# Causal attention with 16 heads on Trainium2: softmax row sums by TensorE over four key tiles in place of GpSimd additions and one product

## What is computed

```python
def _L2_attn_ref(x, w_q, w_kv, w_o, k_weights):      # h = 16 heads, v = 64 values per head
    q = x @ w_q * (1.0 / jnp.sqrt(d))                # (b, 512, 1024) -> (b, 16, 512, 64)
    kv = x @ w_kv                                    # keys and values from one projection
    k = kv * (1.0 + k_weights)
    logits = jnp.einsum('bhik,bhjk->bhij', q, k)
    logits = jnp.where(tril, logits, -1000000.0)     # causal
    a = jax.nn.softmax(logits, axis=-1)
    y = jnp.einsum('bhij,bhjv->bhiv', a, kv)
    return y @ w_o
...
x = _layernorm(x + _L2_attn_ref(x, ...))
```

## Time and profile before

| | us |
|---|---|
| median of 3 runs | 3564.88 |
| lowest and highest of them | 3562.05, 3566.03 |
| profiled execution, its own time | 3560.01 |
| its span in the trace | 3558.3 |
| TensorE matmuls busy | 2880.4 (81%) |
| VectorE busy | 2106.9 (59%) |
| ScalarE busy | 1306.5 (37%) |
| GpSimd busy | 882.6 (25%) |
| first and last exponential of the stage (line 2372) start at | 2013.0 and 2456.9 |

### The profile page before, as it was taken

The page is one execution under the profiler, slowest core; times in us unless marked ns, Lnnn a source line. Parts: engine busy times, 40 slices in busy tenths (PEclk is TensorE's granted clock), DMA queues, the critical chain, the costliest instruction groups (busy, mean ns, idle before and its releaser), DMA issues. The chain is left out here.

```text
span 3558.3 us, 41277 instructions
## 1 busy us (share of the span) xinstructions
PE 2880.4 (81%) x14768; PEld 1337.2 (38%) x14768; DVE 2106.9 (59%) x4175; ACT 1306.5 (37%) x2243; POOL 882.6 (25%) x1147
## 2 busy tenths in 40 slices
PE   4996879665555998879797899997785599699998
PEld 1332434221112443535354434434333233254555
DVE  5874841478777545555555355555667678464444
ACT  2664642333432552020211243332553266355221
POOL 2101100257546103030303254445215200110000
PEclk9997889888777999889899899999786699799999
DMA  5212200100001200000000000000300221220000
GB/s 136 42 28 59 47 19 1 47 0 0 0 0 31 60 12 1 1 1 0 1 1 1 17 1 1 1 1 1 61 12 0 34 42 34 73 51 8 1 1 12
DMA packets 39979, 74.60 MB, mean 21 GB/s; under 512 B 13048, under 2 KB 31916, under 8 KB 35936
## 3 DMA queue, kind: packets, MB, share of 16 engines
q1 hardware_dynamic: 39776, 71.96, 9.3%
HBM read 26.28 MB, written 1.05 MB: 8 GB/s over the span
## 5 line engine op out<-in xcount | busy, mean ns | idle before, releaser
L1630 POOL TENSOR_TENSOR mamba_dbu<-mamba_du,mamba_b 128x512 f32<-128x512 f32 x128 | 256.0, 2033 | 134.1 <-ACT mamba_b L1613 134.1
L1597 PE MATMUL ps<-mamba_hc,weights 128*128 128x512 f32 x256 | 167.1, 745 | 97.1 <-DVE mamba_hc L1655 96.7
L1644 DVE TENSOR_TENSOR_SCAN mamba_h<-mamba_da,mamba_dbu 128x512 f32<-128x512 f32 x128 | 211.3, 1653 | 18.3 <-ACT mamba_da L1618 18.3
L164 POOL TENSOR_SCALAR vareps<-mv 128x4 f32<-128x4 f32 x24 | 6.1, 254 | 760.6 <-DVE mv L1271 463.0
L534 DVE TENSOR_REDUCE L3a_negmax<-ps 128x1 f32<-128x512 f32 x256 | 162.5, 684 | 52.1 <-PE ps L294 51.6
L2310 DVE TENSOR_REDUCE skv_negmax<-ps 128x2 f32<-128x256 f32 (+3 forms) x128 | 105.1, 823 | 147.4 <-PE ps L2158 147.4
L534 DVE TENSOR_REDUCE L0a_negmax<-ps 128x1 f32<-128x512 f32 x256 | 162.5, 684 | 50.1 <-PE ps L294 49.6
L397 ACT ACTIVATE L0a_probs<-ps 128x512 f32<-128x512 f32 x256 | 143.7, 599 | 76.1 <-PE ps L313 74.5
L397 ACT ACTIVATE L3a_probs<-ps 128x512 f32<-128x512 f32 x256 | 143.7, 599 | 74.1 <-PE ps L313 72.5
L2372 ACT ACTIVATE skv_probs<-ps 128x1024 f32<-128x1024 f32 (+3 forms) x128 | 90.1, 704 | 205.3 <-PE ps L2184 205.3
L2045 PE MATMUL ps<-stream,moa_xm 128*128 128x128 f32 x1024 | 153.7, 296 | 1.4 <-DVE moa_xm L2067 1.4
(11 more groups left out here) (624 smaller groups left out, 6776.8 us busy)
## 6 DMA issues: line engine op xcount, KB each, us to landing
stream<-stream SPq DMA_DIRECT2D x32, 192.0 KB
stream<-gate_up_down_in SPq DMA_DIRECT2D x1, 4352.0 KB, 14.0
stream<-value_output_in SPq DMA_DIRECT2D x1, 4096.0 KB, 12.0
stream<-ffn_in SPq DMA_DIRECT2D x1, 2888.0 KB, 9.5
L0a_qs<-L0a_qs SPq DMA_DIRECT2D x16, 128.0 KB
L0x_qs<-L0x_qs SPq DMA_DIRECT2D x16, 128.0 KB
L1x_qs<-L1x_qs SPq DMA_DIRECT2D x16, 128.0 KB
L2x_qs<-L2x_qs SPq DMA_DIRECT2D x16, 128.0 KB
```

What stands on the lines that cost most here:

```text
L1597: pe.matmul(ps[:, 4 + j, :], k.ident, hc[:, (J * n + j) % RING, :], start=n == 0, stop=n == N - 1).then_inc(s["summed"], 1)
L1630: pool.tensor_tensor(dbu[:, i % RING, :], du[:, j, :], bsb[:, n % AHEAD, :], ALU.mult).then_inc(s["dbu_ready"], 1)
L1644: dve.tensor_tensor_scan(out=hs[:, i % RING, :], data0=da[:, i % RING, :], data1=dbu[:, i % RING, :], initial=0.0, op0=ALU.mult, op1=ALU.a ...
```

## The change

`total`, `add_up` and the semaphore `added` go. `sums(R)` now multiplies each of the four key tiles of `probs` by ones, for the queries that the tile reaches, and accumulates in PSUM: eight matmuls in place of two. It waits for `kept` (GpSimd's masking) and not for `added`. It runs in step R+1, behind the last `weigh(R)`, and no longer in step R+2; `copy_sums`, `invert` and `normalize` move up by one step with it. Before it overwrites a buffer of `probs`, ScalarE waits for `summed` in place of `added`.

```diff
--- before.py
+++ after.py
@@ -2101,7 +2101,6 @@
         mparts = sb("mparts", [P, 2, NT, 2, WD], BF16)
         mt = sb("mt", [P, 2, SEQ], BF16)
         probs = sb("probs", [P, 2, 2, NT, SEQ])
-        total = sb("total", [P, 2, 2, SEQ])
         inv = sb("inv", [P, 2, SEQ])
         halves, tri, sel = (wb(k, n).rearrange("p (c n) -> p c n", c=2) for n in ("halves", "tri", "sel"))
         ones = w(k, "const", "one")
@@ -2109,7 +2108,7 @@
         mt_ps = ps[:, M_BANK, :].bitcast(BF16)
 
         with phase(k, "chain", "pool_chain", "cleared", "q_ready", "k_ready", "v_ready", "q_sb", "k_sb", "v_sb", "scores",
-                   "maxed", "split", "mt_ready", "mt_sb", "scoresT", "exped", "kept", "weighed", "z_out", "added", "summed",
+                   "maxed", "split", "mt_ready", "mt_sb", "scoresT", "exped", "kept", "weighed", "z_out", "summed",
                    "sum_sb", "inverted", "normalized", "y_ready", "y_read", "xT_sb", *NORM_SEMS) as (block, s):
             @block.tensor
             def _(pe):
@@ -2200,11 +2199,13 @@
 
                 def sums(R):
 
-                    pe.wait_ge(s["added"], 2 * (R + 1))
+                    pe.wait_ge(s["kept"], NT * (R + 1))
                     take("sum_sb", R + 1)
-                    for a in range(2):
-                        o = WD * a
-                        last = pe.matmul(ps[o:o + WD, M_BANK, :], ones[:, 0:WD], total[:, R % 2, a, :], start=True, stop=True)
+                    for t in range(NT):
+                        for a in range(2):
+                            o = WD * a
+                            last = pe.matmul(ps[o:o + WD, M_BANK, t * P:], ones[:, 0:WD], probs[:, R % 2, a, t, t * P:],
+                                             start=t == 0, stop=t == NT - 1)
                     last.then_inc(s["summed"], 1)
 
                 def project_out(b):
@@ -2236,8 +2237,8 @@
                                 project_k(step + MAKE)
                             elif t == 2:
                                 project_v(step + MAKE)
-                        if t == 3 and 2 <= step < ALL + 2:
-                            sums(step - 2)
+                        if t == 3 and 1 <= step < ALL + 1:
+                            sums(step - 1)
                     if step >= -1 and step % G == G - 1 and step + 1 < ALL:
                         turn_maxima((step + 1) // G)
                     if batch_at(step, OUT_AT) is not None:
@@ -2270,25 +2271,10 @@
                     pool.affine_select(out=at, in_=at, pattern=[[0, 2], [1, P]], compare_op=ALU.is_ge, fill=0.0, base=0,
                                        channel_multiplier=-1).then_inc(s["kept"], 1)
 
-                def add_up(R, a):
-                    pool.wait_ge(s["kept"], NT * (R + 1))
-                    if R >= 2:
-
-                        pool.wait_ge(s["summed"], R - 1)
-                    p, to = probs[:, R % 2, a], total[:, R % 2, a]
-                    pool.tensor_copy(to[:, 0:P], p[:, 0, 0:P])
-                    last = pool.tensor_tensor(to[:, P:], p[:, 0, P:], p[:, 1, P:], ALU.add)
-                    for t in range(2, NT):
-                        chain(last)
-                        last = pool.tensor_tensor(to[:, t * P:], to[:, t * P:], p[:, t, t * P:], ALU.add)
-                    last.then_inc(s["added"], 1)
-
                 for step in range(FIRST, LAST):
                     for t in range(NT):
                         if 0 <= step < ALL:
                             keep_causal(step, t)
-                        if 1 <= step <= ALL and t < 2:
-                            add_up(step - 1, t)
                     R = step + LOOK
                     if 0 <= R < ALL and R % G == G - 1:
                         split(R // G)
@@ -2337,12 +2323,12 @@
                     for t in range(NT):
                         if 0 <= step + LOOK < ALL:
                             maxima(step + LOOK, t)
-                        if 3 <= step < ALL + 3:
-                            invert(step - 3, t)
+                        if 2 <= step < ALL + 2:
+                            invert(step - 2, t)
                         if t == 1 and step + MAKE < ALL:
                             weigh_keys(step + MAKE)
-                    if 3 <= step < ALL + 3:
-                        normalize(step - 3)
+                    if 2 <= step < ALL + 2:
+                        normalize(step - 2)
 
             @block.scalar
             def _(act):
@@ -2367,7 +2353,7 @@
                             if step >= 2 and t == 0:
 
                                 act.wait_ge(s["weighed"], step - 1)
-                                act.wait_ge(s["added"], 2 * (step - 1))
+                                act.wait_ge(s["summed"], step - 1)
                             act.wait_ge(s["scoresT"], i + 1)
                             act.activation(probs[:, step % 2, :, t, t * P:], ps[:, T_BANK:T_BANK + 2, t * P:], ACT.Exp,
                                            scale=scale).then_inc(s["exped"], 1)
@@ -2382,8 +2368,8 @@
                                 act.wait_ge(s["v_ready"], R + 1)
                                 act.copy(v[:, R // NT % 2, R % NT, :, :].rearrange("p r d -> p (r d)"), ps[:, M_BANK, :]
                                          ).then_inc(s["v_sb"], 1)
-                        if t == 3 and 2 <= step < ALL + 2:
-                            copy_sums(step - 2)
+                        if t == 3 and 1 <= step < ALL + 1:
+                            copy_sums(step - 1)
                     if step >= -1 and step % G == G - 1 and step + 1 < ALL:
                         g = (step + 1) // G
                         act.wait_ge(s["mt_ready"], g + 1)
```

## The result

| | before | changed |
|---|---|---|
| median of 4 runs, us | 3565.23 | 3599.14 |
| lowest and highest | 3562.05, 3566.03 | 3596.5, 3606.19 |
| profiled execution, own time (span), us | 3560.01 (3558.3) | 3596.5 (3594.8) |
| stage, from the memset of `skv_mparts` to the first memset of `L2x_ks`, us | 504.3 | 539.1 |
| GpSimd busy, us | 882.6 | 728.1 |

The changed kernel is slower: ratio 1.0101, 95% interval [1.0085, 1.0116]. The stage alone is 34.8 us longer; it also began 1.9 us later (the memset of `skv_mparts` starts at 1982.1 and not at 1980.2), and that part comes from stages which the change does not touch.

What follows compares the result with a forecast made beforehand. TensorE's matmuls were taken to bound the steps, with GpSimd's time free there. Longer blocks +38.9, the new block +3.0 and the stage's end -5.7 made +36.2 us; 3564.9 + 36.2 = 3601.1 us, range 3592 to 3611.

Steps and rivals of the forecast that it cites:

- The bound: Inside the steps: a microsecond of matmul is a microsecond of time, a microsecond of GpSimd is worth nothing.
- The term of 29 blocks: Sums of steps 2 to 30, before step 31's sums: each grows by 1.34 us, +38.9 us.
- The low count: Sums counted by columns: 768 more cost 1.21 us a pair, the lower end, giving 3597.3 us.
- The wait for the copy: Odd steps: TensorE's wait of 0.78 us for ScalarE's copy of the sums stays, whatever the block's length.
- Step 1: End of step 1: a block of sums that was not there before, +3.0 us.
- The end: From step 31's sums to the output projection's end: waits for GpSimd go, full clock, a gain of 5.7 us.
- The sum: Whole kernel: 38.9 + 3.0 - 5.7 = +36.2 us, forecast 3601.1 us.
- Weight loads don't come bare: Rival, in the sums: 12 more loads a pair come bare, 52 us on top, +88 or 3653 us; chance 0.05.
- The gaps before the weight loads: Rival, before loads of `probs`: gaps are hidden waits for GpSimd, 51 us, removal gives -15 or 3550; chance 0.02.
- The idle time of TensorE: Rival, in the stage: new products fill the idle 4%, about 18 us, giving +18 or 3583 us; chance 0.04.
- nothing measurable would happen: Rival, in each step: the change does nothing measurable, needing 1.34 us of TensorE free; chance 0.01.

Runs made afterwards that it cites:

- doubled sums: Changed kernel with every block of sums done twice over: median 3670.49 us, ratio 1.0291.
- the additions kept: Changed kernel with GpSimd's additions put back, result unread, ScalarE waiting for them before overwriting `probs`: median 3601.98 us, ratio 1.0098.
- the run of the end only: Kernel before, but TensorE sums the four key tiles for the last two pairs, without the move by one step: median 3557.36 against 3562.44 us, ratio 0.9987.
- one bfloat16 part: Kernel before, with GpSimd's totals rounded once to bfloat16 and multiplied by ones in one product: median 3551.07 us, ratio 0.9965.
- that without the move: Changed kernel with the sums back in step R+2 and a third buffer of `probs`: median 3602.7 us, ratio 1.0104.
- the run of the move alone: Kernel before, with only the sums and what follows them one step earlier; GpSimd still adds: median 3571.11 against 3565.09 us, ratio 1.0017.
- the two runs with one part: Kernel before with totals rounded to bfloat16, alone (3551.07 us, ratio 0.9965) and with TensorE summing the last two pairs' tiles (3548.98 us, ratio 0.9957).
- the run with parts: Kernel before, with GpSimd also splitting each total into two bfloat16 parts that TensorE multiplies: median 3564.85 against 3562.44 us, ratio 1.0006.

## Why the prediction was right

**The bound.** TensorE's time is paid one for one: doubled sums cost 2.15 us a pair, and 154.5 us less of GpSimd (158 were forecast) bring nothing in the steps, shown from the other side by the additions kept (+0.6 us in all, none of it in the steps).

**The term of 29 blocks.** Taken at 1.34 us each, measured 1.29 to 1.30: 2.25 against 0.96 to the next matmul, and 2.37 against 1.07 to ScalarE's copy. So 37.6 us in place of 38.9. The row it came from, the 2.38 us of the last `weigh`, is 0.06 longer than the same four shapes in the changed kernel, 2.32 in the sums and in the `weigh` at 2501.42 alike. It began after a wait, but that isn't the whole reason: in the run of the end only a `weigh` takes 2.37 right behind another block. The low count, 1.21, compared unlike followers: a block is 0.96 before scores and 0.95 before `weigh` with 512 columns, 2.25 and 2.15 with 1280, and the forecast's 2.17 had sums behind it.

**The wait for the copy.** It stayed at 0.78 us, as forecast. But the reason given, that it is ScalarE's copy "whatever the length of the block", is too wide: with one bfloat16 part the block is shorter and the wait grows to 1.05.

**Step 1.** 3.10 - 0.10 = 3.0 us, as worked out. From the first exponential to step 31's sums it is 444.0 us before (2013.0 to 2457.03) and 484.4 after (2014.9 to 2499.26), +40.4; the two terms give 40.6.

**The end.** -5.8 us for -5.7, with the clock at full. The run of the end only and that without the move confirm both of its parts, the wait for GpSimd and the clock.

**The sum.** 40.4 - 5.8 = 34.6 us, and 0.2 behind the projection, where the clock now falls a little sooner, make the 34.8 of the stage; forecast 36.2. 1.9 us more came from stages before it, so that the total of 36.5 us in the profiled executions (median to median 33.9) is nearer to the forecast than the stage is; that is chance. The time of 3599.14 against 3601.1 lies inside that scatter.

**The rivals.** Weight loads don't come bare: a block now has 16 of them and 2.25 us, and the doubled one costs 2.15 us more. The Trainium skill's rule for the overlap of loads ("TensorE: Matmul & The Clock Gate", Part 3: only if the row group differs) does not describe loads like these, which share all rows and alternate between the two halves of the columns; the measurement decides. The same part also lets the engine pull a load ahead when it goes to the background weight buffer; no row here tells which buffer a load uses. The gaps before the weight loads of `weigh` stayed, though the masking came earlier (before they were 39.3 us in 98 cases). From 2060 to 2420 in the changed kernel:

```profile
PEld ps L2195 <- issue: 35.5, 90, 0.6
```

With the additions kept the same stretch has the same 35.5 us in 90 cases, so these gaps were no waits for GpSimd. The idle time of TensorE absorbed nothing, since it stands behind ScalarE's copy of the sums. That nothing measurable would happen is refused by the ratio's interval.

## What to carry to other kernels

Ask first which engine bounds the steps, and price a trade between engines by that one alone: here 5 us of GpSimd a pair were free and 1.3 us of TensorE were not. Then look at the first and last turns of the pipeline apart, because there the same trade can have the other sign; an edit that is wrong for 30 turns was right for the last two. Where a chain is shortened, name what was hidden behind it, as ScalarE's 0.58 us copy was.

## What I had not expected of the hardware

A wait of TensorE near the end of the stage can cost more than itself. In the run of the move alone the clock was at half after the first wait, of 2.02 us:

```profile
2446.00:2452.00 6.00, 4.55 (x14) 1.30 (x14) 5.10 (x9) 1.74 (x3) 0.78 (x1) 0.50 0.00 0
```

That is its window over 6 us behind the wait, with the columns of the earlier trace rows: granted clock 0.50, 1.2 GHz. But not every wait does it: behind the one of 1.97 us in step 31 of the same run the block of sums takes 1.08 us and `weigh` 2.32, both at full clock, and the half clock in step 30 of the two runs with one part came without a wait of more than 1.05 us in that step. What decides is open. In the run with parts a `weigh` took 4.53 us after a wait of 5.61, and the output projection 10.24 and not 7.41. In every run in which TensorE did not wait for GpSimd at the end, the last `weigh`, the sums and the projection ran at full clock. Of the 3.8 us that the run of the end only gained between step 31's sums and the projection's end (16.70 us and not 20.55), 2.3 are clock (9.67 to 7.41 us of projection) and not waiting.
